# Half-step tables of heads, tails, attentions and feed-forwards written anew in a two-layer sequence kernel

## The reference

```
h = mamba_block(x)                  # x_ssm, z = xn @ in_proj; conv over 4 taps, silu
                                    # delta = softplus(...); h_t = exp(delta A) h_t-1 + delta B x
                                    # y = sum(h C) + x D; residual + (y * silu(z)) @ out_proj
x = x + attention_block(h)          # 4 heads, causal softmax; then silu(xn gate) * (xn up) @ down
x = x + layernorm(gelu(x @ tern(W_fc))) @ tern(W_proj)
x = x + mamba_2(x)                  # as the first, inner width 256, state 16
x = x + top-1 of 8 experts(x)       # router, silu(a) * g @ w2, times the largest probability
```

## Time and profile before

| what | value |
|---|---|
| median of 3 runs | 733.44 us (732.43 to 739.2) |
| profiled execution | 736.92 us |
| its span | 735.1 us |
| mean granted clock of PE in it | 0.919 |
| busy: PE, DVE, ACT, POOL | 596.1, 587.0, 495.3, 420.3 us |

### The profile page before, as it was taken

One profiled execution on the slowest core, in us unless ns is written; L12 is line 12 of the kernel. 1 busy time (PEld: TensorE's weight loads), 2 busy tenths in 40 slices (PEclk: granted clock), 3 DMA queues, 4 the chain that ended last, 5 costly groups with the idle time before them and its releaser, 6 DMA issues. The chain is left out here.

```text
span 735.1 us, 9892 instructions
## 1 busy us (share of the span) xinstructions
PE 596.1 (81%) x3364; PEld 395.2 (54%) x3364; DVE 587.0 (80%) x592; ACT 495.3 (67%) x921; POOL 420.3 (57%) x234
## 2 busy tenths in 40 slices
PE   6686686888988969998698996898677677869995
PEld 2154363456554545545454554554444466659995
DVE  3599989998989759987697889788899899854442
ACT  3859834877598786897878789678966678313231
POOL 0078754555666464735566346675687567445663
PEclk9689879798999889999899997899899899989999
DMA  4670650075005700007400075003800751257771
GB/s 133 261 238 15 238 223 1 0 282 195 25 4 193 284 0 2 1 2 290 186 1 0 1 266 210 1 0 101 361 1 1 263 199 53 67 162 236 220 228 42
DMA packets 35661, 91.63 MB, mean 125 GB/s; under 512 B 7492, under 2 KB 13115, under 8 KB 35611
## 3 DMA queue, kind: packets, MB, share of 16 engines
q1 hardware_dynamic: 34138, 87.93, 34.1%
q0 software_dynamic: 1472, 3.06, 1.5%
HBM read 87.87 MB, written 3.11 MB: 124 GB/s over the span
## 5 line engine op out<-in xcount | busy, mean ns | idle before, releaser
L527 POOL TENSOR_TENSOR hc<-hst,bc 128x1024 f32<-128x1024 f32 x127 | 299.0, 2362 | 164.6 <-DVE hst L1096 78.8
L1108 DVE TENSOR_TENSOR_SCAN hst<-dA,bank 128x1024 f32<-128x1024 f32 x84 | 191.4, 2282 | 2.1 <-PE bank L1760 0.2
L671 ACT ACTIVATE dA<-delta,m_A_s 128x511 f32<-128x511 f32 x256 | 173.2, 712 | 9.1 <-DVE hst L1108 6.0
L1470 PE MATMUL bank<-ident,hc 128*128 128x128 f32 x1016 | 142.8, 289 | 12.8 <-POOL hc L527 12.7
L1470 PEld LDWEIGHTS bank<-ident,hc 128*128 128x128 f32 x1016 | 125.3, 151 | 42.9 <-issue 24.0
L1079 DVE TENSOR_TENSOR bank<-bank,bc 128x1024 f32<-128x1024 f32 x79 | 97.1, 1229 | 10.0 <-DMA bc<-crows 3.7
L1377 PE MATMUL bank<-arena 128*32 128x128 f32 (+6 forms) x466 | 52.6, 361 | 11.9 <-ACT arena L761 6.5
L467 POOL TENSOR_TENSOR du<-delta,xs 128x512 f32<-128x512 f32 x15 | 19.1, 1273 | 71.5 <-DVE delta L1120 71.5
L1096 DVE TENSOR_TENSOR_SCAN hst<-dA,bank 128x512 f32<-128x512 f32 x44 | 53.7, 1220 | 1.5
L1090 DVE TENSOR_TENSOR_SCAN hst<-dA,bank 128x512 f32<-128x512 f32 x44 | 53.5, 1215 | 0.8
L1377 PEld LDWEIGHTS bank<-arena 128*32 128x32 f32 (+3 forms) x466 | 26.5, 141 | 38.9 <-issue 21.5
(11 more groups left out here) (262 smaller groups left out, 1092.8 us busy)
## 6 DMA issues: line engine op xcount, KB each, us to landing
bc<-crows SPq DMA_DIRECT2D x126, 512.0 KB, 9.3
bc<-in_w SPq DMA_DIRECT2D x23, 512.0 KB, 4.0
xin<-in_xT SPq DMA_DIRECT2D x8, 256.0 KB, 4.4
rows_out<-arena SPq DMA_DIRECT2D x1, 1056.0 KB, 6.4
conv<-in_m_cw SPq DMA_DIRECT2D x2, 512.0 KB, 4.5
crows<-prow SPq DMA_DIRECT2D x8, 64.0 KB, 1.6
arena<-rows_out,source POOLq DMA_INDIRECT x23, 3.5
out_rows<-zs,target POOLq DMA_INDIRECT x23
```

Source lines behind the costliest of these rows:

```text
L527: pool.tensor_tensor(hc[:, g % HCRING], hst[:, g % HRING], bc[:, p, 1], ALU.mult) \
L671: act.activation(dA[:, g % RING, j, 1:], delta[:, h, 1:], ACT.Exp, scale=M[mamba_of(c)]["A"][:, h, n:n + 1]).then_inc(sems["dA"], 1)
L1108: dve.tensor_tensor_scan(hst[:, g % HRING].rearrange(flat), dA[:, g % RING].rearrange(flat), bank[:, first_bank:first_bank + 2, :].rearran ...
L1470: last = pe.matmul(bank[:, YB, P * j:P * j + P], hc[:, g % HCRING, n, P * j:P * j + P], ident[:], start=False, stop=s % PAIRS == PAIRS - 1 ...
```

## The change

All tables but PAIRED, A0, F0, A_LAG and SINGLE get new numbers. No line of code, no operation, buffer or wait differs. Most numbers move by one or two half-steps. The moves by name, as entry: before to after.

| table | moves |
|---|---|
| HEAD[1] | sp0 28 to 26, sp1 33 to 32, visit 23 to 21, prow 23 to 21 |
| HEAD[3] | du1 36 to 32, visit 21 to 22, raw1 12 to 13 |
| HEAD[4] | dt1 31 to 33, sp1 31 to 33, delta1 32 to 33, du1 32 to 34, du0 26 to 30 |
| HEAD[5] | delta0 30 to 29, delta1 34 to 35, du1 37 to 32 |
| HEAD[7] | z0 21 to 23, z1 22 to 23, zp0 22 to 24, zp1 27 to 26, xp 26 to 24, du0 26 to 28 |
| TAIL | [2] ycp1 3 to 5, res 6 to 5; [3] ycp1 3 to 2; [4] back0 32 to 30; [7] back0 26 to 31, gate0 32 to 43 |
| A_START | [0][0] 8 to 3; [2][0] 5 to 7, [2][2] 14 to 13, [2][4] 23 to 22; [3][2] 15 to 14 |
| AAT[3] | rec 32 to 31, o 33 to 34, h1 34 to 35 |
| FAT | [0] gelu, hsq, hr 24 to 26; [1] down 17 to 16, scale 26 to 25; [2] gu 10 to 9, fc 18 to 17, proj 31 to 32, x2 32 to 33 |

The diff, cut to the lines that hold most of these:

```diff
...
-TAIL = (dict(ycp1=2, back1=4, gate1=3, out=5, res=6, ycp0=18, back0=31, gate0=32), dict(ycp1=3, back1=4, gate1=5,
-    out=6, res=7, ycp0=19, back0=31, gate0=32), dict(ycp1=3, back1=3, gate1=5, out=3, res=6, ycp0=19, back0=31,
...
+TAIL = (dict(ycp1=2, back1=3, gate1=3, out=4, res=4, ycp0=20, back0=29, gate0=31), dict(ycp1=3, back1=4, gate1=4,
+    out=6, res=6, ycp0=19, back0=31, gate0=32), dict(ycp1=5, back1=3, gate1=5, out=3, res=5, ycp0=19, back0=31,
...
-A_START = ((8, 11, 16, 19, 22, 25), (6, 14, 18, 20, 23, 27), (5, 10, 14, 18, 23, 25), (6, 11, 15, 18, 21, 25))
...
+A_START = ((3, 11, 16, 19, 22, 25), (6, 14, 18, 20, 23, 27), (7, 10, 13, 18, 22, 25), (6, 11, 14, 18, 21, 25))
...
-FAT = (dict(sq=0, var=1, rs=3, nrm=3, gate=6, park=6, xh=9, visit=9, up=9, gu=10, down=14, x1=15, cen=16, cp=16,
-    st=18, rst=19, fc=20, fcp=20, gelu=24, hsq=24, hr=24, scale=25, turn=27, tc=27, proj=31, x2=33), dict(sq=0, var=2,
...
-NSTART = {1: 2, 2: 14, 3: 26}
-LATE_AT = 15
-Z_FIRST = (36, 39)
+FAT = (dict(sq=1, var=1, rs=3, nrm=4, gate=6, park=6, xh=7, visit=9, up=9, gu=10, down=14, x1=15, cen=15, cp=15,
+    st=18, rst=18, fc=20, fcp=20, gelu=26, hsq=26, hr=26, scale=25, turn=27, tc=27, proj=32, x2=34), dict(sq=0, var=2,
...
+NSTART = {1: 1, 2: 16, 3: 24}
+LATE_AT = 11
+Z_FIRST = (34, 35)
...
```

More of the change, by code:

```diff
@@ new lines @@
+TAIL = (dict(ycp1=2, back1=3, gate1=3, out=4, res=4, ycp0=20, back0=29, gate0=31), dict(ycp1=3, back1=4, gate1=4,
+    out=6, res=6, ycp0=19, back0=31, gate0=32), dict(ycp1=5, back1=3, gate1=5, out=3, res=5, ycp0=19, back0=31,
+    gate0=31), dict(ycp1=2, back1=3, gate1=4, out=5, res=7, ycp0=19, back0=30, gate0=30), dict(ycp1=2, back1=3,
+    gate1=4, out=4, res=8, ycp0=19, back0=30, gate0=32), dict(ycp1=2, back1=5, gate1=5, out=5, res=13, ycp0=18,
+    back0=30, gate0=31), dict(ycp1=2, back1=4, gate1=6, out=5, res=8, ycp0=18, back0=29, gate0=34), dict(ycp1=4,
+    back1=8, gate1=17, out=8, res=27, ycp0=17, back0=31, gate0=43))
@@ new lines @@
+HEAD = (dict(raw0=12, park0=5, raw1=12, park1=6, z0=6, zp0=16, z1=17, zp1=28, visit=9, xp=2, prow=16, dt0=24, sp0=30,
+    delta0=28, du0=16, decay=27, dt1=33, sp1=33, delta1=35, du1=33), dict(raw0=5, park0=10, raw1=10, park1=14, z0=19,
+    zp0=19, z1=19, zp1=20, visit=21, xp=21, prow=21, dt0=21, sp0=26, delta0=29, du0=29, decay=31, dt1=30, sp1=32,
+    delta1=34, du1=38), dict(raw0=8, park0=9, raw1=9, park1=13, z0=14, zp0=15, z1=15, zp1=18, visit=20, xp=21,
+    prow=25, dt0=26, sp0=28, delta0=29, du0=26, decay=31, dt1=34, sp1=34, delta1=35, du1=36), dict(raw0=7, park0=13,
+    raw1=13, park1=15, z0=16, zp0=16, z1=16, zp1=21, visit=22, xp=24, prow=24, dt0=25, sp0=25, delta0=27, du0=31,
+    decay=18, dt1=32, sp1=33, delta1=36, du1=32), dict(cen=12, cp=12, var=16, rs=18, xn=16, raw0=20, park0=21,
+    raw1=22, park1=22, z0=24, zp0=25, z1=25, zp1=26, visit=27, xp=27, prow=27, dt0=28, sp0=28, delta0=29, du0=30,
+    decay=29, dt1=33, sp1=33, delta1=33, du1=34), dict(cen=13, cp=14, var=16, rs=18, xn=16, raw0=20, park0=19,
+    raw1=21, park1=23, z0=23, zp0=24, z1=25, zp1=26, visit=27, xp=27, prow=27, dt0=28, sp0=28, delta0=29, du0=30,
+    decay=29, dt1=33, sp1=32, delta1=35, du1=32), dict(cen=12, cp=14, var=14, rs=16, xn=16, raw0=19, park0=19,
+    raw1=23, park1=22, z0=25, zp0=25, z1=26, zp1=26, visit=28, xp=27, prow=28, dt0=28, sp0=28, delta0=30, du0=30,
+    decay=29, dt1=32, sp1=32, delta1=35, du1=36), dict(cen=11, cp=15, var=14, rs=16, xn=15, raw0=18, park0=16,
+    raw1=20, park1=21, z0=23, zp0=24, z1=23, zp1=26, visit=28, xp=24, prow=28, dt0=28, sp0=28, delta0=31, du0=28,
+    decay=23, dt1=34, sp1=34, delta1=37, du1=35))
@@ L77 @@
-NSTART = {1: 2, 2: 14, 3: 26}
-LATE_AT = 15
-Z_FIRST = (36, 39)
+FAT = (dict(sq=1, var=1, rs=3, nrm=4, gate=6, park=6, xh=7, visit=9, up=9, gu=10, down=14, x1=15, cen=15, cp=15,
+    st=18, rst=18, fc=20, fcp=20, gelu=26, hsq=26, hr=26, scale=25, turn=27, tc=27, proj=32, x2=34), dict(sq=0, var=2,
+    rs=2, nrm=3, gate=7, park=7, xh=5, visit=11, up=10, gu=11, down=16, x1=17, cen=17, cp=17, st=19, rst=18, fc=19,
+    fcp=19, gelu=23, hsq=24, hr=24, scale=25, turn=27, tc=28, proj=31, x2=33), dict(sq=0, var=2, rs=3, nrm=4, gate=5,
+    park=5, xh=6, visit=8, up=9, gu=9, down=15, x1=15, cen=16, cp=16, st=17, rst=17, fc=17, fcp=17, gelu=24, hsq=24,
+    hr=24, scale=27, turn=27, tc=27, proj=32, x2=33), dict(sq=2, var=0, rs=2, nrm=2, gate=2, park=4, xh=7, visit=7,
+    up=8, gu=9, down=15, x1=16, cen=17, cp=17, st=18, rst=18, fc=18, fcp=18, gelu=23, hsq=24, hr=24, scale=28,
+    turn=28, tc=27, proj=31, x2=35))
```

33 lines of the change are left out of this document (4 added, 29 removed).

## The result

The changed kernel takes 739.2 us, median of 20 runs (736.19 to 743.41), against 734.75 us for the kernel before in the same comparison (20 runs, 731.06 to 739.2). The ratio is 1.0064 with a 95% interval of 1.0044 to 1.0084: slower by 0.6%, where 727.7 us and a range up to 737.0 had been forecast. Sign and range were both missed. The kernel before took 734.75 us here where the forecast had started from 733.44, the median of 3; of the miss of 11.5 us that is 1.3. The profiled execution has a span of 739.7 us against 735.1.

What follows compares the result with a forecast made beforehand. DVE was taken to set the pace, its idle time being what could be won. Terms of -8.0 us with +2.2 returned gave -5.8: 736.92 to 731.1 us profiled, 727.7 on the median, range 720.5 to 737.

Steps and rivals of the forecast that it cites:

- signs of being right: Named DVE waits gone, shortened or new in blocks 0 to 5, with the b3 t5 loop still costing 5 us or more.
- blocks 0 and 1: Earlier softplus closes two gaps (-1.7 us), attention 0's earlier first pair closes one before the maximum (-1.3): -3.0 us.
- b3 t5, the loop: Queue loop of DVE's gate and PE's out stays; res wins 0.67, later ycp1 delays the gate 1.4: +0.8 us.
- b3 t14 to t24: Block 3: attention 2's moved pairs remove waits of 1.12 and 0.59 us before maxima; silu wait stays: -1.7 us.
- b3 t28 to b4 t7: Earlier down -1.9, later dt1 and delta1 +2.3, earlier ycp1 -3.0, res and norm -0.7: -3.3 us.
- b4 t20 to b5 t0: Earlier gu0 and gu1 only move waits (+0.7), one more fc before scores at t29 (+0.4): +1.1 us.
- block 5, t9 to t12: Later o, h1, x2 and proj put a drive and a scan into DVE's gaps: -1.2 and -0.7, -1.9 us.
- blocks 6 and 7: No net change, 0 us; up to 2 us lost if hc 12's 1.4 us margin ahead of scan 15 is gone.
- The return: A third of the 6.6 us won in blocks 1, 3 and 5 comes back as other waits: +2.2 us.
- rival 1: Gains fall back into other waits, only the softplus gaps stay won, some 1.5 us: 732 us; chance 0.20.
- Rival 2: Slower: PE runs block 4's dt1 stretch at low clock, delta1 waits 12.4 us: 736.6 on the median; chance 0.14.
- Rival 3: PE's idle stretches go, nothing returns, block 3's loop runs at full clock: 726.7, median 723.3 us; chance 0.18.

Runs made afterwards that it cites:

- same: The kernel before run again with nothing changed, a second look at the old order; ratio 0.9985 against the kernel before.
- again: The changed kernel run once more with nothing changed, on the chip of the parts; ratio 1.0067 against the kernel before.
- g_start: The kernel before with only new HEAD[1] sp0 and sp1, A_START[0][0] and AAT[0] up to vc; ratio 0.9963, in a repeat 0.9935.
- r_waits: The changed kernel with seven entries put back (HEAD[0] sp1, TAIL[0] res, HEAD[4] dt1, sp1, delta1, du1, HEAD[5] delta0); ratio 1.0026 against the kernel before.
- d_down: The kernel before with only down of feed-forward 1 one half-step earlier (17 to 16); ratio 1.0021.
- g_gate: The kernel before with only ycp1 of block 3 at half-step 2 in place of 3; ratio 1.0020.
- e_delta: The changed kernel with dt1, sp1, delta1 and du1 of HEAD[4] and delta0 of HEAD[5] put back; ratio 1.0060 against the kernel before.
- f7_after: The changed kernel with two filler products on PE ahead of x_project's wait, at block 7 alone; ratio 0.9993 against the kernel before.

## Why the prediction was wrong, by its own steps

The step that failed is the one that chose the terms: "I went through DVE's idle gaps in the timeline, step by step; those that the tables touch are the terms." The gaps on that list mostly moved as forecast. But six waits that were on no list appeared: 1.81 us (b0 t3), 1.68 (b1 t4), 1.61 (b3 t29), 2.17 (b4 t14), 2.79 (b4 t29) and 1.91 (b6 t31), 12 us in all, against the 5.8 us that were to be won. It did not help that the table in "The change" names 44 of some 190 moved numbers; `res` of block 0 is not among them, and `NSTART` was given no term.

Of the forecast's own signs of being right five of six came true: no wait before delta at b0 t29 and b1 t2, none before the gate at b4 t4, x1 at 1.42 us, 3.81 at b4 t1, and 5.98 in the loop of b3 t5; only h1 and x2 took 3.23 us and not under 2. All of them are places on the old list, so they could not tell that the sum was wrong. Its sign of being wrong did: DVE's idle time did not fall by 4 to 8 us, it rose.

The forecast's terms against the gaps of the changed kernel (DVE's idle time, before to after, from the lines above and the smaller gaps beside them):

| step | forecast | measured |
|---|---|---|
| blocks 0 and 1 | -3.0 | -0.3 (5.4 to 5.1) |
| block 2 | none | +1.6 (6.9 to 8.5) |
| b3 t5, the loop | +0.8, bounds -0.7 to +3 | -0.6 (7.2 to 6.6) |
| b3 t14 to t24 | -1.7 | +1.0 (4.2 to 5.3) |
| b3 t28 to b4 t7 | -3.3 | -3.8 (11.4 to 7.6), then +2.2 at b4 t14 |
| b4 t20 to b5 t0 | +1.1 | +3.0 (9.3 to 12.2) |
| block 5, t9 to t12 | -1.9 | -0.2 (4.6 to 4.4) |
| blocks 6 and 7 | 0 | +1.2 (+2.4 and -1.3) |

These are the first two profiles; by the second ones the rows for blocks 0 and 1 and for block 5 are uncertain by 1 to 2 us (`same` 4.3 and `again` 6.1 in blocks 0 and 1).

**Blocks 0 and 1: mechanism right, its rest missed.** The three gaps named closed, and g_start shows that they stay won. The step that failed is "NSTART, LATE_AT and Z_FIRST move ACT and PE work in block 0, where DVE has no gap for them". DVE had no gap there before, and got one of 1.81 us before delta1, because PE's dt1 now stands behind the product of `NSTART[1]` (read from the trace, see r_waits); and res of block 0, moved from t6 to t4, meets PE's out too early, 1.68 us. I priced the gaps that were there and not the ones that an earlier consumer makes. r_waits shows that 1.68 can be had back.

**Block 3, t5: right within its bounds.** The copy was ready at 258.47 us, not after 261.5, so the loop's lower bound came true. res is not done inside the old gap but ends a gap of its own: 3.87 and 2.11 for 6.62.

**Block 3, t14 to t24: wrong.** "The wait of 2.53 us for the silu table and two silus at t22 stays (`visit` and `gu` are where they were)". It grew to 4.88. The visit is where it was, but DVE arrived 2.5 us earlier in the block: its waits ahead were 1.5 us shorter, and a copy on DVE (L1159) took 0.43 us for 1.84. The silu still ended 65.3 us behind the start of the block (65.4 before). Block 2's visit grew from 1.90 to 3.37, and had no term at all.

**Block 3, t28, to block 4, t7: right as far as it went.** x1 fell by 1.9, delta1 waits 3.81 where 3.4 was worked out, the gate's wait went. The failed step is the first one, "Now `down` follows x_project at once": it left out delta0 behind it, 1.61 us; d_down shows the exchange alone, 2.03 for 2.58. And what was left fell back at b4 t14 (2.17). g_gate shows such a return without any other edit, at b4 t5 to t7: 2.96 of 3.03.

**Block 4, t20, to block 5, t0: a term left out.** The move of delta0 of block 5 to t29 was in the diff and in no term: 2.79 us. e_delta shows that taking it away doesn't help: the maximum behind it takes it over.

**Block 5: the wait went one place on.** h1 fell from 2.04 to 0.77 as forecast. But proj starts at 467.04 us for 465.39, behind an accumulation that itself waits 0.81 us for POOL's hc; I had counted that later start as a gain of 0.7, and x2 rose from 1.70 to 2.46.

**Blocks 6 and 7: the wrong chain.** Block 6 grew by 2.8 us (62.2 to 65.0, in the second looks 62.2 to 64.9), more than any other. "If that margin of 1.4 us is gone" looked at the product hc and at scan 15. What decides is a chain one further back, silu, x_project, row copy, dt0, softplus, delta0. With x_project queued at t24, PE stands idle for longer (3.66 us for 3.03), then runs x_project at the low clock and two accumulations ahead of dt0 instead of one. With the same entries and the clock high (f7_after) the wait before delta0 is 0.21 us and not 1.91; with the old entries and the clock low (last section) it is 1.2 to 1.3. So most of it is the clock. The line of PE in the kernel before, then in the changed one:

```profile
569.01 1.96 PE L1377 MATMUL bank<-xs,m_wx_s 128*96 128x512 f32 x4 [3.03 <-ACT xs L626]
```

```profile
569.69 3.31 PE L1377 MATMUL bank<-xs,m_wx_s 128*96 128x512 f32 x4 [3.66 <-ACT xs L626]
```

**The return.** A third of the 6.6 us was let return. In blocks 3 and 4 it was all of it, which was rival 1's mechanism, but its price, 732 us, was still too low, for it had no term for a consumer that comes too early. Rival 2 had the right sign and the wrong place: the low clock struck not at dt1 of block 4 (the stretch from 338.7 us ran at 1.00 again) but at the head of block 7. Rival 3's clock went the other way in the changed kernel (the loop's turn and `out` took 1.09 and 3.78 us again). That such a gain exists g_start shows, 0.63 and 3.06 us, but under other tables, and the loop's last wait fell by 0.6 us, not by 2.2.

## What to carry to other kernels

When a static order is changed in many places, walk through every moved consumer and ask what it will wait for, also where the profile has no gap; a list of today's gaps can only show gains. A wait removed ahead of a stretch in which another engine is full (here blocks 3 and 4) is worth nothing; moves ahead of slack (blocks 0 and 1) kept roughly what the gaps said, 1.6 to 3.5 us for 3.0. Run moves one at a time on the old order and keep those that win; parts of a coupled order can be slower than either whole, and their prices don't add. Profile the old order twice before putting a difference of a few us down to the change.
